# Score matmuls on 28-row bands between full-height matmuls, in a fused cross-attention and expert layer

## What is computed

```python
q = _split_heads(queries @ Wq + bq)
k = _split_heads(keys @ Wk + bk)
v = _split_heads(values @ Wv + bv)
scores = jnp.einsum('bhqd,bhkd->bhqk', q, k) * scale
attn = jax.nn.softmax(scores, axis=-1)
o = jnp.einsum('bhqk,bhkd->bhqd', attn, v)
...
x = x + jnp.tanh(g_xattn[0]) * _L0_xattn_ref(_layernorm(x, axis=-1), ctx_1024, ctx_1024, ...)
x = x + jnp.tanh(g_ffn[0]) * _L0_ffn_ref(_layernorm(x, axis=-1), ...)
```

## Time and profile before

| | us |
|---|---|
| median of 3 runs | 698.83 (698.7 to 701.12) |
| the profiled execution | 701.08, of it 699.3 are the span of the core |
| setup until the first score matmul | 0 to 74.6 |
| attention, units 0 to 6 (with M) | 74.6 to about 381 |
| attention, unit 7 (no M) | about 381 to 413 |
| router, search of the thresholds | 413 to about 470 |
| experts | the rest |

### The profile page before, as it was taken

How to read it: one execution, slowest core, us unless ns; L and a number is a source line. 1 busy time by engine, 2 the same in 40 slices (tenths; PEclk the granted TensorE clock), 3 DMA queues, 4 the chain that set the end, 5 groups by cost and what they waited for, 6 DMA issues and landing times.

```text
span 699.3 us, 10376 instructions
## 1 busy us (share of the span) xinstructions
PE 588.2 (84%) x3452; PEld 318.1 (45%) x3452; DVE 479.8 (69%) x952; ACT 405.2 (58%) x748; POOL 160.4 (23%) x161
## 2 busy tenths in 40 slices
PE   4875899999999999999999983012999999999992
PEld 4421233323333234332332231002889888988991
DVE  3789977779788797886877014885576786786531
ACT  2554478767778677877677961000555666565551
POOL 3023202002030020560000001003143653463333
PEclk9989899999999999999999995555999999999997
DMA  7500000000000000000001005001135554463322
GB/s 249 185 1 0 1 1 0 2 1 1 1 31 31 1 0 0 30 30 0 1 1 60 1 1 180 0 0 38 53 100 141 121 135 126 103 172 100 61 31 30
DMA packets 23326, 35.39 MB, mean 51 GB/s; under 512 B 3411, under 2 KB 15988, under 8 KB 23156
## 3 DMA queue, kind: packets, MB, share of 16 engines
q1 hardware_dynamic: 17140, 26.45, 11.5%
q0 software_dynamic: 6144, 8.39, 7.1%
HBM read 26.45 MB, written 8.39 MB: 50 GB/s over the span
## 4 chain that ended last, share of the span: by engine, by line
PE 71%; DVE 11%; ACT 7%; issue 4%; POOL 2%; DMA 0%; POOLq 0%; DVEq 0%; ACTq 0%
PE ps L1191 14%; PE ps L1392 13%; PE ps L1399 13%; PE ps L1287 13%; PE ps L1175 9%; ACT probs L609 5%; DVE mhalf L814 4%; DVE ge L988 3%; PE ps L1138 2%; PE ps L1214 1%; PE ps L1226 1%; PE ps L1374 1%; PE ps L1115 1%; PE ps L1220 1%; ACT c L540 1%
## 5 line engine op out<-in xcount | busy, mean ns | idle before, releaser
L814 DVE TENSOR_REDUCE mhalf<-ps 128x1 f32<-128x802 f32 x256 | 247.5, 988 | 62.9 <-PE ps L1175 60.4
L609 ACT ACTIVATE probs<-ps 128x512 f32<-128x512 f32 (+1 forms) x416 | 233.1, 599 | 91.0 <-PE ps L1287 88.5
L1287 PE MATMUL ps<-qfull,kpad 128*128 128x512 bf16 (+1 forms) x416 | 153.0, 384 | 7.5 <-ACT probs L609 2.0
L1175 PE MATMUL ps<-kpad,qrows 128*128 128x401 bf16 x512 | 132.8, 343 | 13.2 <-DVE mhalf L814 11.7
L1191 PE MATMUL ps<-probs,vp 128*32 128x512 f32 (+1 forms) x832 | 110.8, 604 | 1.5 <-ACT osb L529 0.9
L1287 PEld LDWEIGHTS ps<-qfull,kpad 128*128 128x128 bf16 (+1 forms) x416 | 40.1, 99 | 141.2 <-ACT probs L609 120.9
L1079 DVE TENSOR_TENSOR h1l<-hf,h1h 128x512 fp32r<-128x512 f32 x64 | 44.5, 695 | 62.3 <-ACT hf L689 54.6
L688 ACT ACTIVATE h1h<-ps,b1T 128x512 fp32r<-128x512 f32 x64 | 43.9, 686 | 60.6 <-PE ps L1392 60.4
L1399 PE MATMUL ps<-w2h,h1h 128*128 128x256 f32 x256 | 73.8, 288 | 3.3 <-issue 2.6
L1175 PEld LDWEIGHTS ps<-kpad,qrows 128*128 128x128 bf16 (+1 forms) x512 | 46.2, 99 | 59.0 <-DVE mhalf L814 27.2
L1399 PE MATMUL ps<-w2l,h1h 128*128 128x256 f32 x256 | 72.4, 283 | 0.0
(11 more groups left out here) (167 smaller groups left out, 668.6 us busy)
## 6 DMA issues: line engine op xcount, KB each, us to landing
w1raw<-in_L_ffn_w SPq DMA_DIRECT2D x16, 512.0 KB, 4.1
w2raw<-in_L_ffn_w SPq DMA_DIRECT2D x16, 512.0 KB
xs<-in_x SPq DMA_DIRECT2D x4, 512.0 KB, 8.1
out<-xs SPq DMA_DIRECT2D x4, 512.0 KB, 2.7
x_rows<-x SPq DMA_DIRECT2D x4, 512.0 KB, 2.6
ctx_sb<-in_ctx SPq DMA_DIRECT2D x3, 512.0 KB, 6.2
b2b<-in_L_ffn_b SPq DMA_DIRECT2D x1, 1024.0 KB, 12.9
toks<-x_rows,idx_get POOLq DMA_INDIRECT x32
```

The lines of the kernel that those rows point to most:

```text
L609: nc.scalar.activation(probs[0:w, par, hh, :], ps[0:w, score_bank(kt, hh, last_unit), :], ACT.Exp, scale=float(SCALE)).then_inc(s_ex, 1)
L814: nc.vector.tensor_reduce(mhalf[:, j:j + 1], ps[:, b:b + 2, 0:MAXW], AX.XY, ALU.max).then_inc(s_mr, 1)
L1175: last = mm(ps[:, 2 + 2 * (j % 2) + b, 0:MAXW], q, kpad[:, HG * g + hh, lo:lo + MAXW], start=True, stop=True)
L1287: mm(ps[0:w, score_bank(kt, hh, last_unit), :], kpad[:, HG * g + hh, P * kt:P * kt + w], qfull[:, g, :], start=True, stop=True).then_inc(s ...
```

## The change

Two edits, both on PE. The score matmul takes only the 28 rows of its head, of `kpad` as well as of `qfull`. The maximum's matmuls keep 128 rows. Since the rows left out of `kpad` are zeros, the scores are the same. And chunks 1 and 2 are written out on PE instead of looped; the other engines keep their loops.

```diff
+        def head_rows(hh):
+
+            return slice(32 * hh, 32 * hh + ROW_V)
...
-                            mm(ps[0:w, score_bank(kt, hh, last_unit), :], kpad[:, HG * g + hh, P * kt:P * kt + w], qfull[:, g, :],
+                            mm(ps[0:w, score_bank(kt, hh, last_unit), :], kpad[head_rows(hh), HG * g + hh, P * kt:P * kt + w], qfull[head_rows(hh), g, :],
                                start=True, stop=True).then_inc(s_sc, 1)
...
-            with pe.Fori(1, NC - 1) as i:
+            for i in range(1, NC - 1):
                 chunk(i, False, False)
```

## The result

The changed kernel takes **745.29 us** (median of 4 runs, 744.85 to 745.61) against 699.98 of the kernel before in the same session: ratio **1.0648** (95% interval 1.0633 to 1.0664). The forecast was 738.2, with a range of 727 to 765. The profiled execution took 744.85 us, its span is 743.0, which is 43.7 more than before. Medians here are over all runs of a kernel, while ratios leave out a run that is over 1.5% above the fastest of the same kernel, which is so for two of four runs of one experiment, with S and M on 28 rows.

The account below looks back on a forecast made before the run. PE and ACT were taken to bound the attention in turn, within 0.1 us. Switches +39.8, `wo` +1.1 and the last unit -1.5 gave +39.4 us: 738.2 us from the median of 698.83, range 727 to 765.

Parts of the forecast that it names:

- The pacing loop: Attention step: S2, exponentials of S2 and S3, S1, PV set the pace; PE work added there is nearly all time.
- The price of a switch: Between a band and a full-size neighbour on PE: 0.12 us each, bounded by 0.09 and 0.145.
- 332 switches: Count of new changes of cut that cost time in the attention, 39.8 us at 0.12 us each.
- `wo`: Six output-projection steps: four more switches each, but 0.29 us lost beside full-height scores goes; together +1.1 us.
- The last unit: Unit without M: four neighbouring scores may overlap, but ACT binds too; -1.5 us of ACT's 2 us idle given back.
- The clock: Granted clock in the attention: falls if quarter-height matmuls are taken for idleness; about 930 us, chance 0.04.
- The unrolled loop: Chunks 1 and 2 on PE: register operations and branch go, straight code costs no more; 0 us.
- Rival 1: S and M in attention: weights of another cut can't load under the matmul before; 0.195 a switch, 765 us, chance 0.15.
- Rival 2: Bands beside full matmuls: the switch costs nothing, only the last unit gains; 697.3 us, no change, chance 0.10.
- rival 3: Scores on the pacing loop: 28-row results come out sooner, faster by more than 0.5%; 677 us, chance 0.04.
- Rival 4: Attention: the chip takes quarter-height matmuls for idleness and the granted clock falls; about 930 us, chance 0.04.

## Why the prediction was right, point by point

- **The pacing loop** was read rightly. Two-half and three-half steps were forecast to take 3.2 and 3.65 and take 3.16 and 3.60. Units 1 to 4 and 6 follow the count of switches to 0.6 us. With one head banded, units 0 to 6 came within 1.7 and 0.9 us of their counts, both below them.
- **The price of a switch** was mis-sized: 0.12 forecast, 0.10 measured, near the lower bound of 0.09. I took half of what PV costs on both sides (0.23). In front of PV the rows had 0.09, close to what a switch measured; the 0.14 behind it made the half too large. That this surplus is PV's own is my reading, and no run isolates it. 332 switches are 33.2 us instead of 39.8.
- **`wo`** between bands: S, `wo` and the next S were forecast to lose 0.29 and lose 0.40. In the changed profile S and `wo` start together, and the next S follows 0.97 later instead of 1.37:

```profile
411.32 0.39 PE L1291 MATMUL ps<-qfull,kpad 28*128 28x512 bf16 x1
411.32 1.12 PE L1218 MATMUL ps<-wo_sb,onT 32*128 32x256 f32 x4
412.29 0.38 PE L1291 MATMUL ps<-qfull,kpad 28*128 28x512 bf16 x1
```

  With four switches at 0.10 in each of the six steps they cost 0.0 instead of 1.1. The part that wasn't forecast is that `wo` runs beside an S on other rows. With scores on 64 rows it doesn't, and the 0.40 is gone.
- **The last unit**: forecast -1.5, measured -0.3 with bands there alone. The step that failed was to count ACT's idle time as something that quicker scores give back. ACT is idle 2.6 us in it with bands as well. Its longest wait, 1.21 us for a score that stands behind the router's matmul (1.88 us) on PE, is as long with bands (399.90) as without (400.33).
- **The clock** was the largest miss. I gave it 0.04, as all or nothing, since "M and PV are most of PE's time and stay". That held in the steady stretch and only there: the clock stayed low after PE's pause at the start and fell again near two waits, and I had read the clock of the steady stretch alone. What the units lose beyond their switches is 3.3 us in unit 0 and 4.4 in unit 5; unit 7 loses 1.7 (28.4 against the 26.7 of the run with bands there alone), and 0.9 stand before unit 0, where the start varies by itself. That is 9.4 to 10.3 us. These are remainders; the run with full-height scores in unit 0 gives 2.8 for the 3.3.
- **The unrolled loop** costs nothing, as written.
- **Rival 1**, a switch of 0.195, is out by the distances in the timeline. Its mechanism is half right: the load of M no longer runs under the S. But load and pause together cost 0.10, not 0.09 + 0.10. Rival 2 is out by the same distances; rival 3 too: the first exponential of a step comes 0.42 us after S2 as before (148.49 to 148.91 in the changed kernel). Rival 4 came true in small, by its own sign, a granted clock under 1.00 before 413 us.

The sum of the parts: 33.2 + 0.0 - 0.3 + 10.3 = 43.2 of 43.7 us. The forecast was 39.4, with 6.6 too much at the switches, 1.1 too much at `wo`, 1.2 too much gained in the last unit and nothing for the clock. That its total is only 4.3 us short is luck: what was too much at the switches and `wo` stood in for most of the clock.

## What to carry to other kernels

A matmul on fewer rows is a matter of its neighbours. Between matmuls of the same cut it pays no switch here and can run beside one on other rows; between matmuls of another cut it pays 0.10 us on each side, so count the changes of cut on the pacing path, not the matmuls. Change the whole run of neighbours or none of it, and then look at the granted clock, first of all where PE comes out of a pause: with S and M both on 28 rows, and no switch between them, the time rose by 83 us and the mean clock fell to 0.742.

## What the runs showed of the hardware

- The change of cut costs 0.10 us at full clock, for bands of 28 and of 64 rows alike (S to M 0.31 and 0.32 us, before 0.22). Across it the weights of M are loaded when M starts (148.80), and no longer 0.01 us after the S before it starts (140.99). Beside a matmul of 124 rows there is no such cost (0.23).
- A score on 28 rows and `wo` on 32 others start together (411.32); one on 64 rows and `wo` don't (0.32 us apart).
- PE busy 5.00 of 5 us with scores on 28 rows had 0.50 from 75 to 89 us (to 87 in a second profile, to 83 with scores on 64 rows); busy 4.16 of 5 us with full ones it was at 1.00. With scores and maximum on 28 rows the clock was at 0.50 through 160 to 180 us with PE busy 18.64 of 20, on 64 rows it held at 1.00 from 94 to 412 us, once it had come back.
- The clock stayed at 1.00 over a pause between full matmuls (1.02 us near 300 before) and fell after the same pause between bands (1.34 us near 330 after). The two pauses aren't equally long, so the part of the rows in this one wasn't isolated. All four profiles with bands of 28 or 64 rows between full matmuls from unit 1 on have this dip, after waits of 1.32 to 1.39 us.
- Weight loads of 28 rows take 92 to 93 ns where those of 128 rows took 98: the height hardly matters to them.
